# Cross attention: turned x for the queries, by TensorE or by VectorE blocks and DMAs

## What is computed

```python
qh = (q @ Wq.T + bq).reshape(B, S, H, D_K).transpose(0, 2, 1, 3)
scores = jnp.einsum('bhqd,bhkd->bhqk', qh, kh) / np.sqrt(D_K)
scores = jnp.where(mask, scores, -1000000000.0)
weights = jax.nn.softmax(scores, axis=-1)
out = jnp.einsum('bhqk,bhkd->bhqd', weights, vh)
return out.transpose(0, 2, 1, 3).reshape(B, S, D_MODEL) @ Wo.T + bo
...
x = _layernorm(x + _L0_xattn_ref(x, ctx_1024, ctx_1024, ...))
x = _layernorm(x + _L0_ffn_ref(x, ...))
```

## Time and profile before

| | us |
|---|---|
| median of 3 timed runs (2677.78 to 2683.57) | 2683.56 |
| the profiled execution's own time | 2683.64 |
| its span in the trace | 2681.8 |
| PE busy | 2556.6 |
| DVE busy | 1915.6 |
| POOL busy | 866.7 |
| ACT busy | 749.1 |

### The profile page before, as it was taken

How to read it: one execution, slowest core, us unless ns; L and a number is a source line. 1 busy time by engine, 2 the same in 40 slices (tenths; PEclk the granted TensorE clock), 3 DMA queues, 4 the chain that set the end, 5 groups by cost and what they waited for, 6 DMA issues and landing times. The chain is left out here.

```text
span 2681.8 us, 36822 instructions
## 1 busy us (share of the span) xinstructions
PE 2556.6 (95%) x13053; PEld 1575.2 (59%) x13053; DVE 1915.6 (71%) x3262; ACT 749.1 (28%) x1103; POOL 866.7 (32%) x900
## 2 busy tenths in 40 slices
PE   8999998999999898999988879999999999999998
PEld 4444544555555444454544447777777777777775
DVE  4788403666667436777778858888888888888886
ACT  1111223333332235666668621111110111111100
POOL 2222203555455346676767711111111111111000
PEclk9999999999999999999999979999999999999999
DMA  5444130000000143343444421111111111111111
GB/s 175 146 151 171 52 98 35 1 0 1 1 1 1 33 103 98 98 103 95 106 105 134 139 95 36 45 45 45 46 46 44 46 43 43 43 43 46 38 39 36
DMA packets 269604, 175.94 MB, mean 66 GB/s; under 512 B 104912, under 2 KB 235344, under 8 KB 268399
## 3 DMA queue, kind: packets, MB, share of 16 engines
q1 hardware_dynamic: 238742, 148.59, 19.3%
q10 hardware_dynamic: 30680, 24.98, 3.3%
HBM read 90.51 MB, written 52.43 MB: 53 GB/s over the span
## 5 line engine op out<-in xcount | busy, mean ns | idle before, releaser
L2099 PE MATMUL bank<-tiles,tl_XQT 128*128 128x512 f32 (+1 forms) x768 | 328.1, 570 | 0.8 <-issue 0.8
L2104 PE MATMUL bank<-tiles,tl_XQT 128*128 128x512 f32 (+1 forms) x768 | 317.9, 557 | 0.0
L2116 PE MATMUL bank<-tiles,tl_HT 128*128 128x512 f32 x682 | 304.2, 602 | 5.0 <-DMA tl_HT<-tl_tmp 5.0
L2099 PEld LDWEIGHTS bank<-tiles,tl_XQT 128*128 128x128 f32 x768 | 233.5, 310 | 72.6 <-issue 15.8
L2104 PEld LDWEIGHTS bank<-tiles,tl_XQT 128*128 128x128 f32 x768 | 236.7, 308 | 65.9 <-issue 0.5
L2116 PEld LDWEIGHTS bank<-tiles,tl_HT 128*128 128x128 f32 x682 | 219.2, 324 | 75.7 <-issue 10.9
L1403 POOL TENSOR_SCALAR_AFFINE_SELECT tiles<-tiles 128x512 f32<-128x512 f32 x256 | 182.7, 716 | 170.1 <-ACT tiles L1630 154.4
L2179 ACT ACTIVATE tl_HQ<-bank 128x512 f32<-128x512 f32 (+1 forms) x96 | 53.9, 562 | 580.4 <-PE bank L2099 545.7
L2046 POOL TENSOR_TENSOR tl_rs<-tl_ve,mhalf 128x1 f32<-128x1 f32 x29 | 15.9, 548 | 537.1 <-DVE tl_ve L2258 537.1
L1730 DVE SCALAR_TENSOR_TENSOR tiles<-tiles,bank 128x1024 f32<-128x1024 f32 (+1 forms) x128 | 141.7, 1148 | 18.8 <-PE bank L1506 18.7
L1408 POOL TENSOR_SCALAR_AFFINE_SELECT tiles<-tiles 128x512 f32<-128x512 f32 x224 | 152.6, 681 | 0.0
(11 more groups left out here) (301 smaller groups left out, 4701.3 us busy)
## 6 DMA issues: line engine op xcount, KB each, us to landing
tl_HT<-tl_tmp SPq DMA_DIRECT2D x248, 44.0 KB, 2.0
tl_HT<-tl_tmp ACTq DMA_DIRECT2D x248, 44.0 KB, 2.0
fp_weights<-space_quant ACTq DMA_DIRECT2D x33, 256.0 KB, 2.5
X<-in_x SPq DMA_DIRECT2D x8, 1024.0 KB, 10.7
v<-tiles SPq DMA_DIRECT2D x32, 256.0 KB, 2.4
unit_g<-tiles SPq DMA_DIRECT2D x32, 256.0 KB, 2.4
unit_gT<-tiles SPq DMA_DIRECT2D x128, 64.0 KB, 2.1
la_GN<-unit_g SPq DMA_DIRECT2D x128, 64.0 KB, 2.0
```

The lines of the kernel that those rows point to most:

```text
L2099: mm = e.matmul(bank[(2 * q) % 3][:, 0:w], chunk(XQT[n % 2], c), WgT[q][:, :, c, :], start=(c == 0), stop=(c == C - 1))
L2104: mm = e.matmul(bank[(2 * q + 1) % 3][:, 0:w], chunk(XQT[n % 2], c), WuT[q][:, :, c, :], start=(c == 0), stop=(c == C - 1))
L2116: mm = e.matmul(bank[DOWN][:, :], chunk(HT, q), WdT[:, q, :], start=(q == 0), stop=(q == IC - 1))
```

## The change

The first eight tiles of x (two groups) are turned as before, by PE and ACT. From the ninth tile on VectorE's block transpose turns the tile from `X` into a buffer `XB` (two of them). That instruction turns each 32x32 block in its place, so the blocks stand where they stood. SyncE then moves them: 16 DMAs a tile, each of 32 partitions x 4 runs of 32 floats (128 bytes), put token block i and feature block j into partitions 32j to 32j+31 and columns of `XT`, which has the same layout as before. `x_turned(s+8)` stands last in VectorE's slot; `x_moved(n)` waits for it and for the queries that last read the buffer; `query` waits for the moves of all tiles of its group by two semaphores (`d_xt`, even and odd tiles). The transposes of x on PE and ACT's copies are gone for 24 tiles, and waits that they needed are dropped or bounded at eight tiles.

```diff
--- before.py
+++ after.py
@@ -871,6 +871,9 @@
             "x2T_mm", "x2T", "l_mm", "biased3", "tanh", "sum3", "stats3", "mean3", "var3", "rstd3", "x3", "mask_float", "mask_fill"))
 
         XT, QT = w.XT, w.QT
+
+        XB = [sb(f"XB{n}", [P, D]) for n in range(2)]
+        s_xt, d_xt = sem("x_turned"), [sem(f"xT_moved{n}") for n in range(2)]
         RS = 3
         SM = [sb(f"SM{n}", [P, W]) for n in range(RS)]
         PT, AT, XL = sb("PT", [P, H // 2, P]), w.AT, w.XL
@@ -884,7 +887,10 @@
 
         turn = lambda n, i: 5 + (3 * n + i) % 2
 
+
+        BY_PE = 2 * B
         x_bank = lambda n: n if n < B else XTB
+        later = lambda n: BY_PE <= n < NT
         x_tile = lambda n: k.x_tile(n % B, n // B)
         there = lambda n: 0 <= n < NT
         SLOTS = range(-2 * B, NT + 5)
@@ -897,12 +903,25 @@
                             a["mask"].rearrange("(n p) s -> p n s", p=P)).then_inc(s_mu.sem, 16)
                 for t, n in ((bo, "L0_xattn_bo"), (lb, "L0_ffn_bias")):
                     e.dma_start(t[:, :], rows_of(a[n])).then_inc(s_lb.sem, 16)
+                def x_moved(n):
+                    g, at = n // B, n % B * P
+                    e.wait_ge(s_xt.sem, s_xt.at(n - BY_PE + 1))
+                    e.wait_ge(s_q.sem, s_q.at(C * (g - 1)))
+                    for i in range(4):
+                        for j in range(4):
+                            e.dma_start(XT[g % 2][32 * j:32 * j + 32, :, at + 32 * i:at + 32 * i + 32],
+                                        XB[n % 2][32 * i:32 * i + 32, :].rearrange("p (c j t) -> p j c t", c=C, j=4)[:, j]
+                                        ).then_inc(d_xt[n % 2].sem, 16)
+
 
                 WgT, WvT, bg = k.local_weights
                 e.wait_ge(k.d_folded, 16)
                 e.dma_start(WgT[:, :, :], chunked(a["L1_attn_Wg_T"])).then_inc(s_next.sem, 16)
                 e.dma_start(WvT[:, :, :], chunked(a["L1_attn_Wv_T"])).then_inc(s_next.sem, 16)
                 e.dma_start(bg[:, :], rows_of(a["L1_attn_bg"])).then_inc(s_next.sem, 16)
+                for s in SLOTS:
+                    if later(s + 2 * B):
+                        x_moved(s + 2 * B)
                 e.wait_ge(s_next.sem, s_next.at(48))
 
             @block.gpsimd
@@ -928,7 +947,8 @@
                 def add_bias(n):
                     if n == 0:
                         e.wait_ge(s_lb.sem, s_lb.at(32))
-                    e.wait_ge(s_t.sem, s_t.at(n + 1))
+                    e.wait_ge(s_t.sem, s_t.at(min(n + 1, BY_PE)))
+                    e.wait_ge(s_xt.sem, s_xt.at(n - BY_PE + 1))
                     e.tensor_tensor(x_tile(n), x_tile(n), bo[:, :], ALU.add).then_inc(s_xb.sem, 1)
 
                 for s in SLOTS:
@@ -955,21 +975,22 @@
                     mm.then_inc(done.sem, 1)
 
                 def transpose_x(n):
-                    e.wait_ge(s_xe.sem, s_xe.at(n - 11))
                     if n > B:
                         e.wait_ge(s_tc.sem, s_tc.at(n))
                     transposed(x_bank(n), x_tile(n), s_t)
 
                 def transpose_x2(n):
                     e.wait_ge(s_x2.sem, s_x2.at(n + 1))
-                    e.wait_ge(s_tc.sem, s_tc.at(min(n + 12, NT)))
+                    e.wait_ge(s_tc.sem, s_tc.at(BY_PE))
                     e.wait_ge(s_xe.sem, s_xe.at(n))
                     transposed(XTB, x_tile(n), s_xl)
 
                 def query(i):
 
                     g, m = i // C, i % C
-                    e.wait_ge(s_tc.sem, s_tc.at(B * g + B))
+                    e.wait_ge(s_tc.sem, s_tc.at(min(B * g + B, BY_PE)))
+                    for d in d_xt:
+                        e.wait_ge(d.sem, d.at(256 * (B // 2) * (g - 1)))
                     s = i - B
                     e.wait_ge(s_qe.sem, s_qe.at(i - 1))
                     e.wait_ge(s_a2.sem, s_a2.at(s - 2))
@@ -1023,7 +1044,7 @@
                     mm.then_inc(s_l.sem, 1)
 
                 for s in SLOTS:
-                    if there(s + 2 * B):
+                    if 0 <= s + 2 * B < BY_PE:
                         transpose_x(s + 2 * B)
                     if there(s - 2):
                         transpose_p(s - 2)
@@ -1045,11 +1066,10 @@
                 four = lambda x: x.rearrange("p (n t) -> p n t", n=C)
 
                 for s in SLOTS:
-                    if there(s + 2 * B):
+                    if 0 <= s + 2 * B < BY_PE:
                         n = s + 2 * B
                         e.wait_ge(s_t.sem, s_t.at(n + 1))
-                        e.wait_ge(s_q.sem, s_q.at(C * (n // B - 1)))
-                        e.activation(XT[(n // B) % 2][:, :, (n % B) * P:(n % B + 1) * P], four(bank[x_bank(n)][:, :]), ACT.Copy).then_inc(s_tc.sem, 1)
+                        e.activation(XT[n // B][:, :, (n % B) * P:(n % B + 1) * P], four(bank[x_bank(n)][:, :]), ACT.Copy).then_inc(s_tc.sem, 1)
                     if there(s - 2):
                         n = s - 2
                         e.wait_ge(s_pt.sem, s_pt.at(n + 1))
@@ -1136,6 +1156,10 @@
                     e.tensor_tensor(y, TH[:, :], y, ALU.add).then_inc(s_a3.sem, 1)
                     statistics(n, y, st3, mv3, ve3, s_a3, s_t3, s_m3, s_v3, s_r3)
 
+                def x_turned(n):
+                    e.wait_ge(d_xt[n % 2].sem, d_xt[n % 2].at(256 * ((n - BY_PE) // 2)))
+                    e.transpose(XB[n % 2][:, :], x_tile(n)).then_inc(s_xt.sem, 1)
+
                 e.wait_ge(s_bq.sem, s_bq.at(16))
                 e.tensor_scalar(bqs[:, :], bq[:, :], SC, None, ALU.mult).then_inc(s_bqs.sem, 1)
                 e.wait_ge(s_lb.sem, s_lb.at(32))
@@ -1155,6 +1179,8 @@
                     if there(s - 2):
                         attended(s - 2)
                         normal(s - 2, mv2, rs2, s_r2, s_x2)
+                    if later(s + 2 * B):
+                        x_turned(s + 2 * B)
 
 
 FULL = P + 1
```

## The result

The changed kernel takes 2767.45 us (median of 4 runs, 2767.28 to 2767.64) against 2683.11 us before (4 runs): a ratio of 1.0319, 95% interval 1.0301 to 1.0337. It is 84 us slower; 2772.6 was forecast. The span of the profiled execution grew from 2681.8 to 2765.9 us.

The account below looks back on a forecast made before the run. PE was taken to bound the stage, its waits paid in full. 2683.6 us plus 84 of pauses plus 14 of slow clock less 9 saved gave 2772.6 us; own range 2756 to 2787, 8-in-10 range 2745 to 2805.

Parts of the forecast that it names:

- the first slots: Slots 2 and 3, where PE waits for POOL and VectorE anyway: removing transposes of x saves only another 0.4 us.
- PE is the bound and pauses are paid in full: Steady part of the changed stage: PE busy 40.00 of 40 us, so whatever makes it wait is paid in full.
- The pause, 14.0 us six times: PE at query 4g's first matmul waits for moves landing at 21.5 instead of 7.5; groups 2 to 7, 84 us.
- lateness of the turned tile: Block transpose stands last in VectorE's slot, so the tile is turned 10.05 us after the scores.
- It is the last tile of a group: Only tile 4g + 3, turned at the end of VectorE's slot 4g - 5, delays query 4g; the other three cost nothing.
- The clock, 14 us: Query matmuls behind each PE pause run at a lower clock: 2.3 us each, six times, 14 us (11 to 17).
- The saving, 9 us: PE's transposes of x removed: 0.44 us in each of slots 4 to 23, 8.7 us, plus another 0.4 earlier.
- the case in which it costs next to nothing: First rival, SyncE's issues: only the late block transpose and one landing remain, 4.7 us six times, 2717 us; 6%.
- the one with 1.0: Rival, SyncE's queue: an issue takes 1.0 us, pauses total 146 us, 2835 us; 2787 and above counts; 12%.
- The wait was paid six times, not once: Rival judged here: PE, once set back 14 us, stays behind VectorE, so one wait only, 2691 us; 5%.
- That the transfers are hidden: Rival, at query 4g: tiles land before the query asks, no wait is left, 9 us gained, 2675 us; 3%.
- The skill's rules: DMA moves: about 50 ns dispatch makes 16 issues some 0.8 us; 512-byte runs asked for line rate, SBUF to SBUF exempt.

Follow-up runs that it names:

- version one slot earlier: Changed kernel with every tile's block transpose and moves one loop slot earlier (tile n in slot n - 9): 2671.6 us, ratio to before 0.996.
- mid-slot: Changed kernel with the block transpose ahead of `shifted` in the same VectorE slot instead of last: 2722.48 us, ratio to before 1.0151.
- half the DMAs: Changed kernel with 8 of the 16 DMAs a tile, feature blocks 0 and 1 only, half of each tile not moved: 2739.95 us, ratio to before 1.0215.
- filled pause: Changed kernel with 16 unread matmuls of 512 columns on PE ahead of each group's first query from the third group on: 2754.61 us, ratio to before 1.0274.
- two slots earlier: Changed kernel with every tile's block transpose and moves two loop slots earlier (tile n in slot n - 10): 2672.43 us, ratio to before 0.9965.

## Why the prediction was right, and by how much its terms were off

The mechanism is the one forecast. That the total was only 5 us too high is in part luck. In the traces the pauses and the clock cost 2.6 us more than forecast (84.7 and 15.9 against 84 and 14), the first slots gave back 2.4 more (2.8 against 0.4), and 5.2 us came from parts of the program that the edit does not touch.

- *PE is the bound and pauses are paid in full.* Right: 83.7 us of pauses and a slow clock behind them account for the 100.5 us by which the changed kernel's stretch exceeds that of the version one slot earlier (535.2 - 434.6): 83.7 + 15.9 = 99.6. The last microsecond is how a pause is counted: from the end of `transpose_p`, 1.04 us after its start, while an unhindered query begins 0.87 after it; six times 0.17 is 1.0.
- *The pause, 14.0 us six times.* 13.85 to 13.99, 83.7 in total, 84 forecast. Its parts were off by 0.1 to 0.3 us each. That lateness of the turned tile is one part is shown by mid-slot (7.7 us earlier, pause 7.7 less); that the issues are another by half the DMAs (5.15 us less for 8 of them, with half the bytes). Of the two prices for an issue, the moves between two places in SBUF (0.62) were the right row, not the stores with the same run length (0.49).
- *It is the last tile of a group.* Right, shown by the version that turns only this tile on PE.
- *The clock, 14 us.* 15.9: the eight matmuls took 5.75 to 6.46 us instead of 3.60, 37.5 - 21.6. The single figure of 2.3 for each pause was 0.35 too low. The filled pause shows that this part is real and separate.
- *The saving, 9 us.* In the steady slots it is what was said (8.3 to 8.4 in the stretch, and 0.4 in slot 4). In the first slots I allowed 0.4. The version one slot earlier reaches slot 4's `transpose_p` 66.5 us after the stage's first transpose, before it took 69.3 (395.09 to 464.42, slot 4 beginning at 463.99): 2.8 us less. This term was too small in the traces, but 1.7 of the 2.8 are the clock: the matmuls that took 5.37 us in the earlier trace rows take 3.67 in the changed kernel. That is not a sure gain of the edit. In the trace of the version with runs of 512 bytes, which differs from the changed kernel only in the moves, they took 5.37 again behind the same wait, and slot 4's `transpose_p` came 68.9 us after the first transpose (the 20 first transposes were slower too, 4.50 us), 0.4 less than before. The other eight traces of edited kernels have 3.67, and there is one trace of the kernel before, so how much of it belongs to the edit stays open. By the medians the versions without a pause gain 9.2 to 11.1 us.

PE's timeline of the changed kernel, the stage's first transposes, those matmuls, slot 4's `transpose_p`, and the start of the next stage; then those matmuls in the version with runs of 512 bytes:

```profile
394.13 2.38 PE L974 MATMUL bank<-ident,X 128*128 128x128 f32 x20 [1.99 <-PEq L104]
...
445.67 3.67 PE L998 MATMUL bank<-space_T 128*128 128x512 f32 x8 [2.71 <-DVE X L1145]
...
459.38 1.04 PE L1015 MATMUL bank<-ident,xl_SM 128*128 128x128 f32 x8
...
994.53 1.09 PE L1587 MATMUL bank<-ident,X 128*128 128x128 f32 x4 [5.31 <-PEq L104]
```

```profile
447.61 5.37 PE L998 MATMUL bank<-space_T 128*128 128x512 f32 x8 [2.70 <-DVE X L1145]
```

- *What remains.* 92.1 in the stretch, less 2.8 in the first slots, makes 89.3. Slot 4 began another 2.2 sooner in this execution: its 20 first transposes took 2.38 us at full clock, where the kernel before and four of the variants took 4.03 or 4.04 and began 1 us later, so this belongs to the execution and not to the edit. Behind the stage 3.0 us more were given back (84.1 - 87.1); no instruction there changed, and from the next stage's first transposes to the end the ten traces take between 1771.4 and 1778.7 us (1774.3 before, 1771.4 in the changed kernel), so 3.0 lies within what executions differ by.
- *The rivals.* An issue costs 0.64 us, so the case in which it costs next to nothing is out; so is the one with 1.0. The wait was paid six times, not once, and each `masked` waits for PE, 17.73 us in the slot with the pause. That the transfers are hidden came true only when they were started a slot sooner.
- *The skill's rules.* The Trainium skill, "DMA: Bandwidth & Descriptors", section "Why small descriptors are slow", exempts transfers from SBUF to SBUF, and the runs of 512 bytes agree: 2770.2 against 2767.45 us. The about 50 ns for a DMA's dispatch stand in the section "Anatomy of one DMA", which describes a DMA issued from GpSimd and gives no interval between issues. Taken as the price of an issue on SyncE's queue, as the first rival took it, the figure does not hold: the interval is 0.64 us here.

The changed kernel one slot earlier takes 2671.6 us, 0.4% below the kernel before and 3.5% below the changed one; two slots earlier (2672.4) and the last tile by PE (2673.2) cannot be told from it. The idea of the change was worth 9 to 11 us, its place in the loop cost about 100.

## What to carry to other kernels

When a step on an engine is replaced by block transpose and DMAs, price the chain, not the bandwidth: where the producer stands in its engine's own slot, plus the number of DMAs times the issue interval, plus one landing, against the point at which the consumer asks. If the sum is later than that, start it one turn of the loop earlier before changing anything else; that needed no new buffer here. And where PE is the bound, add to each pause what the lower clock costs behind it: 2.3 to 2.6 us on average for the pauses of 6 to 14 us in this kernel.

## What was unexpected on the hardware

- A pause of PE costs about as much slow clock when it is 6.3 us long (14.0 us over six) as when it is 14 us long (15.9 over six), and 13.7 us over six when it is 8.8 us. A pause of 2.7 us at the same matmuls cost nothing in the changed kernel (3.67 us) and 1.7 us in the version with runs of 512 bytes (5.37).
- Behind equal pauses the eight matmuls of the query differ by 1.7 us in one execution (5.06 to 6.75 us in the mid-slot version), so one such row is a poor measure of the cost; the sum of six is needed.
- The interval between SBUF-to-SBUF DMAs on SyncE's queue is 0.64 us when ScalarE's queue is silent, and was 0.62 with both at work. The transfers there have another shape, so this is no clean comparison, but it gives no sign that the two queues slow each other's issue. Sharing the 16 issues between the two queues was not tried.
